# The last phase's first feed-forward layer: planes by thirds through two PSUM banks, and four back banks

## The reference

```python
x = x + _L0_conv_ref(_ln_c(x), ...)      # clusters of tokens
t = _to_tokens(x)
t = t + _L0_ffn_ref(_ln_t(t), ...)
x = _from_tokens(t, x)
x = x + _L1_conv_ref(_ln_c(x), ...)      # depthwise convolutions, a 1x1, times the normed input
t = _to_tokens(x)
t = t + _L1_ffn_ref(_ln_t(t), ...)       # the part whose code is changed
x = _from_tokens(t, x)
```

```python
def _qlinear(x, W, b):
    y = q_acc(jnp.einsum('bsk,nk->bsn', q_mul(x), q_mul(W)))
    return q_acc(y + q_mul(b))
h = jax.nn.relu(_qlinear(x, W1, b1))
y = _qlinear(h, W2, b2)
```

## Time and profile before

| what | value |
|---|---|
| median of 3 runs | 4172.24 us (4168.22 to 4173.44) |
| profiled execution, its own time | 4171.88 us |
| its span, first to last instruction | 4170.3 us |
| PE busy in the span | 3300.1 us (79%) |
| DVE busy | 3017.9 us (72%) |
| ACT busy | 2708.9 us (65%) |
| POOL busy | 1410.4 us (34%) |

### The profile page before, as it was taken

One profiled execution on the slowest core, in us unless ns is written; L12 is line 12 of the kernel. 1 busy time (PEld: TensorE's weight loads), 2 busy tenths in 40 slices (PEclk: granted clock), 3 DMA queues, 4 the chain that ended last, 5 costly groups with the idle time before them and its releaser, 6 DMA issues. The chain is left out here.

```text
span 4170.3 us, 80301 instructions
## 1 busy us (share of the span) xinstructions
PE 3300.1 (79%) x26660; PEld 2535.7 (61%) x26660; DVE 3017.9 (72%) x7852; ACT 2708.9 (65%) x5762; POOL 1410.4 (34%) x1892
## 2 busy tenths in 40 slices
PE   5777777777777777767769999999788888888887
PEld 5656556555565555655549999999644444444443
DVE  4888888888888888888842222222388888888887
ACT  2677777776777777767752222222188888888887
POOL 3555555555555555555310000000012211222221
PEclk8888888888888888888769999999899999999998
DMA  3133232332333323322236656666666666666662
GB/s 68 41 82 82 67 77 70 78 83 62 77 75 77 79 62 77 77 77 62 58 103 165 166 160 167 162 163 167 167 178 180 182 178 179 182 174 175 172 179 74
DMA packets 733893, 490.42 MB, mean 118 GB/s; under 512 B 420796, under 2 KB 712956, under 8 KB 721276
## 3 DMA queue, kind: packets, MB, share of 16 engines
q1 hardware_dynamic: 733564, 486.32, 44.3%
HBM read 284.42 MB, written 201.33 MB: 116 GB/s over the span
## 5 line engine op out<-in xcount | busy, mean ns | idle before, releaser
L1790 POOL TENSOR_SCALAR C_var<-C_st 128x16 f32<-128x16 f32 x64 | 13.2, 207 | 1733.2 <-DVE C_st L178 1733.2
L1331 PE MATMUL B_ps_row<-B_g,B_z 128*128 128x128 f32 x4608 | 555.9, 277 | 0.6 <-ACT B_g L1363 0.6
L1331 PEld LDWEIGHTS B_ps_row<-B_g,B_z 128*128 128x128 f32 x4608 | 532.2, 193 | 0.7 <-ACT B_g L1363 0.7
L361 ACT ACTIVATE A_h<-A_hid 128x512 f16<-128x512 f32 x768 | 426.6, 591 | 67.7 <-PE A_hid L348 64.0
L1424 DVE TENSOR_TENSOR B_mid<-B_ps_row,B_row_bias 128x512 f32<-128x512 f32 x192 | 132.7, 691 | 458.0 <-PE B_ps_row L1331 448.0
L166 POOL TENSOR_TENSOR A_rstd<-A_var,A_expo 128x16 f32<-128x16 f32 x128 | 454.2, 3548 | 23.8 <-POOL A_var L163 23.6
L178 DVE BATCH_NORM_STATS2 A_st<-A_xT 128x6 f32<-128x192 f32 x1536 | 442.9, 349 | 24.8 <-ACT A_xT L826 11.6
L1461 ACT ACTIVATE C_q<-C_xT,C_shift,C_rstd 128x96 fp8e5<-128x96 f32 x1024 | 392.0, 458 | 39.1 <-POOL C_shift L1797 38.9
L369 DVE TENSOR_SCALAR A_hq<-A_h,A_b 128x512 f16<-128x512 f16 x768 | 250.1, 363 | 198.9 <-ACT A_h L361 194.0
L307 ACT ACTIVATE C_h<-C_hid 128x1536 f16<-128x1536 f32 x256 | 370.5, 1447 | 19.1 <-PE C_hid L272 10.9
L856 ACT ACTIVATE A_xc<-A_xT,A_shift,A_rstd 128x96 f32<-128x96 f32 x1024 | 379.1, 456 | 0.0
(11 more groups left out here) (162 smaller groups left out, 7677.8 us busy)
## 6 DMA issues: line engine op xcount, KB each, us to landing
A_xq<-in_x SPq DMA_DIRECT2D x32, 1536.0 KB, 8.9
x_scratch<-A_xT SPq DMA_DIRECT2D x64, 768.0 KB, 3.2
x_scratch<-A_x3h SPq DMA_DIRECT2D x64, 768.0 KB, 5.4
B_z<-x_scratch SPq DMA_DIRECT2D x96, 512.0 KB, 5.0
y_scratch<-B_y SPq DMA_DIRECT2D x96, 512.0 KB, 3.7
C_x3q<-x_scratch SPq DMA_DIRECT2D x32, 1536.0 KB, 9.2
C_y3q<-y_scratch SPq DMA_DIRECT2D x32, 1536.0 KB, 15.6
C_xT<-x_scratch SPq DMA_DIRECT2D x64, 768.0 KB, 15.0
```

The lines of the kernel that those rows point to most:

```text
L361: act.activation(self.h16[:, k % 2, j * CH:(j + 1) * CH], self.hid2[n % 2][:], ACT.Copy).then_inc(ev["h16"], 1)
L1331: m = pe.matmul(ps_row[h][:, b * P:(b + 1) * P], z[c.buf(NB)][:, h * HB + b, d:d + W], g[c.buf(2)][:, d, :], start=(d == 0), stop=(d == 2))
```

## The change

`RowFeedForward`, the feed-forward part of phase C, now inherits from `SplitFeedForward` instead of `FeedForward`. So it uses that class's `pe_hidden`, `act_hidden` and `dve_hidden`, which work on plane j of chunk k, numbered n = 3k + j: the plane goes to bank n % 2, and its matmul waits until plane n - 2 has been copied. The three banks of `hid` become two, and the bank that comes free is the fourth back bank. On PE, the third plane is written behind `mix`:

```diff
-class RowFeedForward(FeedForward):
+class RowFeedForward(SplitFeedForward):
...
-        self.hid = ctx.enter_context(nc.psum_tensor(phase + "hid", [P, NJ * CH], F32))
+        self.hid2 = [ctx.enter_context(nc.psum_tensor(phase + f"hid{p}", [P, CH], F32)) for p in range(2)]
...
-                                        hidden=NK, h16=NK, relu=NK, hq=NK, y16=NK, yb=NK, out=NK, pw_full=NK,
+                                        hidden=NJ * NK, h16=NJ * NK, relu=NK, hq=NK, y16=NK, yb=NK, out=NK, pw_full=NK,
...
-        back = Ring(back_uses, [ctx.enter_context(nc.psum_tensor(f"C_bbank{p}", [P, 512], F32)) for p in range(3)])
+        back = Ring(back_uses, [ctx.enter_context(nc.psum_tensor(f"C_bbank{p}", [P, 512], F32)) for p in range(4)])
...
-                        ff.pe_hidden(pe, i, s)
+                        ff.pe_hidden(pe, i, s, 0)
+                        ff.pe_hidden(pe, i, s, 1)
                     if q.real and s < NK:
                         mix(i, s)
+                    if i.real and s < NK:
+                        ff.pe_hidden(pe, i, s, 2)
...
-                        ff.act_hidden(act, i, s)
+                        for j in range(NJ):
+                            ff.act_hidden(act, i, s, j)
```

## The result

The changed kernel takes 4152.49 us (median of 5 runs, 4150.77 to 4154.17) against 4172.24 before: 19.7 us less, ratio 0.9953, interval 0.9938 to 0.9967. Its profiled execution took 4150.77 us, span 4149.2.

What follows compares the result with a forecast made beforehand. No engine was full: ACT bounded slots 3 to 6, the chain `out`, `c_turn`, `pe_y`, ACT's y bounded slots 8, 1 and 2. Saving 0.84 us in 31 quads (26) plus about 1 from 4172.2 gave 4145, stated 4146; range 4120 to 4188.

Steps and rivals of the forecast that it cites:

- Smaller ACTIVATEs: ACT's copy of `hid`: three ACTIVATEs of 512 columns cost 0.10 us more than one of 1536, 26 us over 256 chunks.
- Slots 3 to 6 "even": Slots 3 to 6, norm to norm: 4.11 us instead of 4.10, with no slack left.
- ACT takes it back: Rival: a third costs 0.10 more in slots 2 to 6 and 0, leaving 0.24 a quad, 4165; 0.23 with another rival.
- the steps: One quad worked through from slot 6 to slots 3 to 6 in six steps of gains, ending at 0.84 us a quad.
- `y` no longer behind `c_turn`: With four back banks the wait on `out` moves to `pe_y`, taking 0.45 us out where `out` ends last.
- step 5: Slot 2: norm only 0.21 us earlier, but y of chunk 1 is ready, 0.90 idle gone: 1.2 earlier.
- Step 4: Slot 1: PE holds `turn`, `c_turn` and `pe_y` until the third plane's matmul is out; ACT's y only 0.42 us earlier.
- Step 6: Slot 3: q8 awaits the norm (0.18), thirds cost 0.19, so 0.84 us a quad is left; slots 4 to 6 keep it.
- The clock "as it is": The lower granted clock's mean price stays at 0.72 us a quad, bounds 0 and 1.8.
- calmer clock: Rival: the shorter idle in slot 8 keeps the full clock, 48 us won, 4124; chance 0.12.
- The slow stretch as the slower side: Rival: at 1.2 GHz the third plane waits for a longer `mix`, also in slot 1: 26 us slower, 4198; chance 0.20.
- The signs named: Trace after: `pe_y` waits for `out`, ACT's wait for it about 60 us, slots 4 to 6 at 4.10, quads at 34.1.

Runs made afterwards that it cites:

- The three-bank kernel: Thirds through three single hid banks and three back banks, all three matmuls ahead of `mix`, run beside the kernel before: 4126.09 us, ratio 0.9885.
- the kernel with three back banks: The changed kernel with its back ring set from four banks to three again, thirds through two hid banks kept: 4174.99 us, ratio 1.0003.
- the pair with held clock: Four unread 512-column matmuls added in slot 8, to the kernel before (4157.22 us) and to the changed kernel (4143.81 us).

## Why the prediction was right, and where it was not

The forecast was 4146 in 4120 to 4188, faster; measured were 4152.5. The gain is 19.7 where 26 were worked out. The sign and the range held, but two terms of the sum were off and leaned against each other: the order of work gave 13 and not 26, and the clock, put at nothing, gave the rest. That the time came out near 4146 is therefore in part luck; 13 alone would have been 4159.

- **Smaller ACTIVATEs, 0.10.** Right: 0.11 with the split copy alone. The Trainium skill (ScalarE: Activation LUTs, What ACT_TABLE_LOAD costs) would have given 0.19, an estimate from its figures, and with it slots of 4.29; the measurement does not agree, at 4.21.
- **Slots 3 to 6 "even", 4.11.** Mis-sized: 4.16, half of what the rival "ACT takes it back" feared. `q8c` to the first plane took 0.50, not 0.48, and first plane to norm 1.56, not 1.53. The three-bank kernel puts the bank's wait at 0.12 a slot. Four slots and slot 7 (3.58, not 3.50) lose about 0.3 against the steps, the larger part of the gain that is missing.
- **`y` no longer behind `c_turn`, 0.45.** Right for slot 8: 0.44 by the kernel with three back banks. Wrong in step 5, where I let it free y of chunk 1 in slot 2: that kernel has no fourth bank and the same 7.04 and 4.16. The 0.90 idle of the earlier trace rows went, but through the earlier `out`, and through a norm that came later.
- **Step 4, PE's order in slot 1.** Right in kind and size: norm to y 4.39 against 4.4 by the steps. What the steps did not show is how dear it is: beside three hid banks 1.13 of 7.04, of which 0.69 comes back in slot 3.
- **Step 6, 0.84 a quad.** It is 0.42. The sum of the misses is 0.12 in slot 2's distance, 4 x 0.06 and 0.08: 0.44.
- **The clock "as it is", 0.72.** Wrong: 0.31. The "calmer clock" was a rival at 0.12 and half of it came true. By the two windows' sums the clock gave 31 x 0.41 = 12.7 us; by the medians, 19.7 less the 13.4 of the pair with held clock, it gave 6. With three back banks the price was still 0.59 and 21 of 28 windows were disturbed, so it is the fourth bank that calmed the clock; it shortens the longer idle of slot 8 from 1.33 to 0.96, and the quad by 0.46, and which of these does it is open. The 28 windows are 23.2 shorter and the profiled execution 21.1, so some of the first figure was lost outside them; which of the two is nearer I can't say from one profile each.
- **The slow stretch as the slower side.** It did not come. The Trainium skill (TensorE: Matmul & The Clock Gate, A second HAM failure mode: psum-queue depth-cycling) tells of a kernel whose clock goes up and down with its cycling through PSUM banks, and I held that against this change. The runs here do not agree: two hid banks in turn with three back banks have 21 of 28 windows disturbed, where the kernel before has 22. The dips that are left in the changed kernel are regular, one in four or five quads. The sum of this rival was wrong too: its terms for the second stretch are 0.9 and 0.8 a quad, so 31 x 1.7 = 53 us and not the 26 of 31 x 0.85.
- **The signs named.** Held: the wait before `pe_y` in place of `c_turn`'s, ACT's wait for it at 59 (about 60), VectorE's wait for h somewhat lower (67.8 from 82.5), the clock not under 0.95. Missed: 4.10 in slots 4 to 6, quads of 34.1. ACT busy 83 more by its durations held (768 x 0.592 - 370.5 = 84); its busy time, which counts an overlap once, rose by 36 only. These are its two lines on the page of the profile (group: count, total us, mean ns):

```profile
PE 3270.8 (79%) x26660; PEld 2521.2 (61%) x26660; DVE 3025.8 (73%) x7852; ACT 2745.2 (66%) x6274; POOL 1425.2 (34%) x1892
...
L361 ACT ACTIVATE C_h<-C_hid 128x512 f16<-128x512 f32 x768 | 426.1, 592 | 15.0 <-PE C_hid L348 7.7
```

By group it is 426.1 instead of 370.5, or 56 more: one overlap of 0.11 in each three copies makes 256 x 0.11 = 28 of the difference to 84. In slots 3 to 6 the first copy now also starts 0.09 before `q8c` ends, where it started behind its end before; that is part of the other 20.

## What to carry to other kernels

A wait on an engine that works in order costs all that is queued behind it. So ask of each buffer's next use what stands behind its wait, and try the order of two neighbours before spending banks: y ahead of `c_turn` won 48 us with no bank at all, the fourth bank 22 (4174.99 to 4152.49), bought with a wait in the first layer that costs 0.93 us a quad, or 49 us (4174.99 to 4126.09). Judge such edits by the undisturbed period and the distance of one engine's marks, slot by slot, and only then by the total, in which the clock may hide or double the effect.

## What the runs showed of the hardware

- The lower granted clock (1.2 GHz) follows a short idle of PE, but not every time. The same two idles in slot 8, 0.93 and 1.33, gave no disturbed window of 28 in a kernel with a quad of 34.10, 12 at 34.46 and 22 at 34.99; these kernels differ in more than the quad's length, and idles of 1.19 and 0.68 at 33.50 gave 13. Four unread matmuls in the idle took the low clock away, or nearly, in three kernels, and won 16 us in the kernel before, 9 in the changed one and 18 in the one with whole planes and y first. What exactly decides is open.
- The price of a small edit on ScalarE was multiplied by that: +0.67 a quad from the split copy came out as 35 us, of which 21 are the work.
- Copies of 512 columns that follow each other on ScalarE start 0.475 us apart, and one of 1536 takes 1.447. Between the start of such a copy and that of the matmul that waits for it lie 0.62 to 0.65 us.
